# Two transposing transfers of a graph kernel, each made in two halves, with a product that waits for each half

## The chip, the cores and the metric

The kernel runs on one core of a Trainium2 chip. The metric is the device time of one execution in microseconds; the median of three executions of the kernel before is 1985.3 us (1983.23 to 1985.93). The engines are TensorE (matrix products), VectorE (DVE), ScalarE (ACT), GpSimd (POOL) and SyncE (SP). In this kernel SP issues every transfer.

## What is computed

128 independent graphs of 128 nodes with 512 features, in two layers, each a residual around a pre-normalised layer:

```python
# layer 0
h = max(layernorm(x), 0)
x = x + L0(h)          # D^-1/2 (A + I) D^-1/2 (h @ W + b)
# layer 1
h = max(layernorm(x), 0)
x = x + L1(h)
# L1: two hypergraph convolutions with a layer norm between them
h = relu(Dn * H (Be * H^T (h @ W1^T)) + b1)     # 512 -> 1024 features
h = layer_norm(h, gamma, beta)                  # this is hn
y = Dn * H (Be * H^T (h @ W2^T)) + b2           # 1024 -> 512 features
```

A is the adjacency matrix, H its nonzero pattern, Dn and Be the inverse degrees of nodes and of hyperedges. The step that the change touches is `h @ W2^T`: hn is 128 nodes x 1024 features, W2^T is 1024 x 512.

## The kernel before

Every float32 operand of a product is split into a float16 high part and a float16 low part, and three products stand for one: high x high, high x low, low x high. The helper `with_weights` (matmuls at L403) does this for a product with a weight matrix: three blocks, and within each one product per block of 128 features. For W2 there are eight such feature blocks, so 24 products of 128x128 by 128x512 that accumulate in the bank `ps_u`.

A product needs its left operand with features on the partitions, while hn is made with nodes on the partitions. So hn's two parts are transposed by transfers from SBUF to SBUF:

- ACT makes `hn_hi` (L675, `do_hn_hi`), DVE makes `hn_lo` (L984, `do_hn_lo`), each 128x1024 in one buffer. Both wait until the previous graph's transfer has read the buffer.
- SP issues one transposing transfer for each (L294, helper `transposed`, called by `do_trh` and `do_trl`) into `hnT_hi` and `hnT_lo`, which have a slot for even and one for odd graphs. Each slot has its semaphore, raised by 16 when the transfer has landed.
- TensorE's `do_U` waits for the high transfer ahead of its first product, and inside `with_weights`, by the argument `low`, for the low transfer ahead of the third block of eight.
- ACT and DVE evacuate `ps_u` into `uh` (L681) and `ul` (L998), and `do_Y2` (L445 to L447) multiplies by the graph's propagation matrix.

Layer 0 has the same form with half the width: `h0T_hi` and `h0T_lo` are transposed 128x512 transfers, made by the same helper, and `do_Y0` multiplies them by W.

The graphs are a software pipeline. In a steady step k TensorE works on T1 of graph k-1, Y0 of graph k, Y2 of graph k-3, two small products, Y1a, Z0 and Y1b, and last on U of graph k-2. The step function of each engine writes its order out by hand; the loop `steady` is unrolled and covers graphs 6 to 121. The opening and the end have orders of their own, also written by hand. SP's order in a steady step is: high transfer of h0 (k+1), high and low transfer of hn (k-2), low transfer of h0, store of the output (L321), load of x (L275), load of adj (L271). Each engine takes its instructions strictly in this order, and waits are on semaphores. In the opening SP's order around graph 1 is `do_tr0l(4); do_trl(1); do_trh(1); do_ldX(7); do_ldA(8); do_st(0); do_tr0h(5)`: there the low transfer of hn goes first.

Of the kernel before, what the change touches and what calls it, by code (L numbers as in the profile page):

```python
# [5 lines left out]
def bass_adjacency_prenorm_two_layer_gnn_kernel(  # L6
# [28 lines left out]
    DH = W1T.shape[1]  # L35
    CH = 512
# [23 lines left out]
    with ctx:  # L60
        def sb(name, shape, dt=F32):
            return ctx.enter_context(nc.sbuf_tensor(name, shape, dt))

        def sem(name):
            return ctx.enter_context(nc.semaphore(name))
# [31 lines left out]
        q = sb("q", [128, 2])  # L97
# [28 lines left out]
        hn_hi, hn_lo = sb("hn_hi", [128, DH], F16), sb("hn_lo", [128, DH], F16)  # L126
        hnT_hi, hnT_lo = sb("hnT_hi", [128, 2 * DH], F16), sb("hnT_lo", [128, 2 * DH], F16)
# [39 lines left out]
        s_wh = [sem(f"W{n}_hi_blocks") for n in range(3)]  # L167
        s_wl = [sem(f"W{n}_lo_blocks") for n in range(3)]
# [1 line left out]

        s_x = [sem(f"x_loaded_{m}") for m in range(4)]
        s_adj = [sem(f"adj_loaded_{m}") for m in range(4)]
        s_trh = [sem(f"hn_hi_transposed_{m}") for m in (0, 1)]
        s_trl = [sem(f"hn_lo_transposed_{m}") for m in (0, 1)]
        s_st = [sem("out_stored_0"), sem("out_stored_1")]

        s_at, s_ahat, s_ht = sem("adjT_in_psum"), sem("ahatT_ready"), sem("HT_and_count_ready")
# [28 lines left out]
        s_u, s_uh, s_ul = sem("u_in_psum"), sem("u_hi_ready"), sem("u_lo_ready")  # L206
# [6 lines left out]
        def at_step(i, k, want):  # L213
            return isinstance(i, int) and k == want
# [3 lines left out]
        def wait(eng, s, i, g):  # L218

            if not isinstance(i, int) or g >= 0:  # L220
                eng.wait_ge(s, upto(i, g))

        def settled(eng):

            eng.wait_ge(s_const, 1)
# [6 lines left out]
        def upto(i, g):  # L232

            return i + (g + 1) if isinstance(i, int) else count[g + 1]
# [15 lines left out]
        def wait_transposed(eng, pair, i, g):  # L250

            if not isinstance(i, int) or g >= 0:
                eng.wait_ge(pair[g % 2], i * 8 + 16 * (g // 2 + 1))
# [9 lines left out]
        def _(sp):  # L263
# [26 lines left out]
            def transposed(dst, g, src, loaded):  # L290

                width = src.shape[1]
                slot = dst[:, g % 2 * width:(g % 2 + 1) * width].rearrange("p (c r) -> p c r", r=128)
                sp.dma_start_transpose(slot, src[:, :]).then_inc(loaded[g % 2], 16)  # L294

            def do_trh(g, i=0):
                settled(sp)
                sp.wait_ge(s_hnh, upto(i, g))
                wait(sp, s_u, i, g - 2)
                transposed(hnT_hi, g, hn_hi, s_trh)  # L300

            def do_trl(g, i=0):
                settled(sp)
                sp.wait_ge(s_hnl, upto(i, g))
                wait(sp, s_u, i, g - 2)
                transposed(hnT_lo, g, hn_lo, s_trl)

            def do_ldA(g, i=0):
                wait(sp, s_at, i, g - 4)
# [26 lines left out]
            def step(i, k):  # L336
                do_tr0h(k + 1, i)
                do_trh(k - 2, i)
                do_trl(k - 2, i)
                do_tr0l(k + 1, i)  # L340
                do_st(k - 4, i)
                do_ldX(k + 4, i)
                do_ldA(k + 4, i)
# [22 lines left out]
            load_row(b1_all, b1, s_rows)  # L366
            do_tr0h(1); do_tr0l(1); do_ldA(4); do_ldX(4); do_tr0h(2); do_tr0l(2); do_ldX(5); do_ldA(5)
            do_trh(0); do_trl(0); do_ldX(6); do_tr0h(3); do_tr0l(3); do_ldA(6); do_tr0h(4); do_ldA(7)
            do_tr0l(4); do_trl(1); do_trh(1); do_ldX(7); do_ldA(8); do_st(0); do_tr0h(5); do_tr0l(5)
            do_trh(2); do_trl(2); do_ldX(8); do_trh(3); do_ldX(9); do_ldA(9); do_trl(3); do_tr0h(6); do_st(1)  # L370
            do_tr0l(6)
# [13 lines left out]
        def _(pe):  # L385
# [6 lines left out]
                    mm = pe.matmul(ps[:, f], lhs_lo[:, f], rhs_hi, start=False, stop=True)  # L392
                return mm

            def with_weights(ps, t_hi, t_lo, w_hi_, w_lo_, blocks, cols, first=None, low=None):

                for n, (t, w) in enumerate(((t_hi, w_hi_), (t_hi, w_lo_), (t_lo, w_hi_))):
                    if low is not None and n == 2:
                        wait_transposed(pe, *low)
                    for j in range(blocks):  # L400
                        if first is not None and n < 2:
                            pe.wait_ge(first[n], j + 1)
                        mm = pe.matmul(ps, t[:, j * 128:(j + 1) * 128], w[:, j, cols],  # L403
                                       start=(n == 0 and j == 0), stop=(n == 2 and j == blocks - 1))
                return mm
# [43 lines left out]
            def do_Y1a(g, i=0):  # L449
                pe.wait_ge(s_t1h, upto(i, g))  # L450
                pe.wait_ge(s_t1l, upto(i, g))
                pe.wait_ge(s_t1h, upto(i, g))
                pe.wait_ge(s_t1l, upto(i, g))
                with_weights(Y1[0][:, :], t1h, t1l, w1h, w1l, KI, slice(0, CH),
                             first=(s_wh[1], s_wl[1]) if at_step(i, g, 0) else None).then_inc(s_y1[0], 1)

            def do_Y1b(g, i=0):
                pe.wait_ge(s_t1h, upto(i, g))
                pe.wait_ge(s_t1l, upto(i, g))
                wait(pe, s_z[1], i, g - 1)  # L460
                with_weights(Y1[1][:, :], t1h, t1l, w1h, w1l, KI, slice(CH, 2 * CH),
                             first=(s_wh[1], s_wl[1]) if at_step(i, g, 0) else None).then_inc(s_y1[1], 1)
# [27 lines left out]

            def do_U(g, i=0):
                cols = slice(g % 2 * DH, (g % 2 + 1) * DH)
                wait_transposed(pe, s_trh, i, g)
                wait(pe, s_uh, i, g - 1)
                wait(pe, s_ul, i, g - 1)
                if at_step(i, g, 0):
                    pe.wait_ge(s_wsum[2], 1)
                with_weights(ps_u[:, :], hnT_hi[:, cols], hnT_lo[:, cols], w2h, w2l, KH, slice(0, DIN),
                             first=(s_wh[2], s_wl[2]) if at_step(i, g, 0) else None, low=(s_trl, i, g)).then_inc(s_u, 1)

            def do_Y2(g, i=0):
                r = g % 4
# [22 lines left out]
            def step(i, k):  # L525
                do_T1(k - 1, i)
                do_Y0(k, i)
                do_Y2(k - 3, i)
                do_AT(k + 2, i)
                do_P(k, i)  # L530
                do_Y1a(k - 1, i)
                do_Z0(k, i)
                do_Y1b(k - 1, i)
                do_U(k - 2, i)
# [18 lines left out]
            beta_row(range(6, 8)).then_inc(s_vps, 1)  # L553
            do_Y1a(0); do_Y1b(0); do_Y0(2); do_AT(4); do_P(2); do_T1(1); do_Z0(2); do_Y1a(1); do_Y1b(1)
            do_U(0); do_T1(2); do_Y0(3); do_Y1b(2); do_Y2(0); do_AT(5); do_Z0(3); do_P(3); do_Y1a(2); do_Y0(4)
            do_U(1); do_T1(3); do_AT(6); do_P(4); do_Z0(4); do_Y2(1); do_Y1b(3); do_Y1a(3); do_Y0(5); do_U(2)
            do_T1(4); do_P(5); do_Z0(5); do_AT(7); do_Y2(2); do_Y1b(4); do_Y1a(4); do_U(3)
            steady(pe, ENG.PE, step)
# [13 lines left out]
        def _(act):  # L572
# [95 lines left out]
            def do_hn_hi(g, i=0):  # L668
                m = g % 2
                act.wait_ge(s_ln2, upto(i, g))  # L670
                act.wait_ge(s_h[0], upto(i, g))
                act.wait_ge(s_h[1], upto(i, g))
                wait(act, s_hnl, i, g - 1)
                wait_transposed(act, s_trh, i, g - 1)
                act.activation(hn_hi[:, :], h[:, :], ACT.Identity, bias=nm2[:, m:m + 1], scale=sc2[:, m:m + 1])\  # L675
                   .then_inc(s_hnh, 1)

# [10 lines left out]
            def step(i, k):  # L688
                do_ha(k - 1, i)
                do_hb(k - 1, i)  # L690
                do_xh(k, i)
                do_xh_hi(k, i)
                do_h0_hi(k + 2, i)
                do_uh(k - 2, i)
                do_t1h(k, i)
                do_hn_hi(k - 1, i)
                do_h0(k + 2, i)
                do_rsum(k + 4, i)
                do_yh(k + 1, i)
                do_A_hi(k + 2, i)  # L700
                do_vq(k - 1, i)
                do_P_hi(k + 1, i)
# [50 lines left out]
        def _(dve):  # L753
# [226 lines left out]
            def do_hn_lo(g, i=0):  # L980
                dve.wait_ge(s_hn, upto(i, g))
                dve.wait_ge(s_hnh, upto(i, g))
                wait_transposed(dve, s_trl, i, g - 1)
                dve.tensor_tensor(hn_lo[:, :], hn[:, :], hn_hi[:, :], ALU.subtract).then_inc(s_hnl, 1)  # L984

            def do_out(g, i=0):
# [32 lines left out]
            def step(i, k):  # L1019
                do_yv(k, i)  # L1020
                do_hn_lo(k - 2, i)
                do_yl(k, i)
                do_h0_lo(k + 1, i)
# [347 lines left out]
```

## Time and profile before

| what | value |
|---|---|
| median of three executions | 1985.3 us (1983.23 to 1985.93) |
| the profiled execution, its own time | 1986.17 us |
| its span, first to last instruction | 1984.4 us |
| TensorE busy | 1961.7 us, 99% |
| DVE busy | 1727.7 us, 87% |
| POOL busy | 1249.4 us, 63% |
| ACT busy | 1083.7 us, 55% |
| W2's products (three groups of 1024) | 243.2 + 242.3 + 241.9 us |
| transposing issues of hn | 128 high, 128 low, 3.1 and 3.3 us to landing |
| mean granted TensorE clock | 0.998 |

The chain of work that ended last lies on TensorE for 98% of the span. A product of 128x128 by 128x512 is shown as 379 ns long, but products overlap: in an unbroken stream the next one starts 0.216 us after the last. So starts, not durations, are to be compared. "To landing" is counted from the start of the issue on SP to the moment at which the transfer's semaphore is complete.

### The profile page before, as it was taken

The numbers are of one execution on the slowest core, as the hardware profiler recorded it, in microseconds if no ns is written. First come the engines' busy times: TensorE is split into PE (matmuls) and PEld (weight loads), VectorE is DVE, ScalarE is ACT, GpSimd is POOL, SyncE is SP. The second block draws the span as 40 slices with busy tenths as digits, with TensorE's granted clock in tenths as the row PEclk, the third lists the DMA queues.
The fourth block names the chain that finished last, engine by engine and source line by source line (L and its number), as shares of the span: only waits on it lengthen the run. The fifth ranks groups of instructions, "written<-read, shape, count | busy, mean of one in ns | idle before, by whom it ended". The sixth has DMA issues, their size and how long they took to land.

```text
span 1984.4 us, 41182 instructions
## 1 busy us (share of the span) xinstructions
PE 1961.7 (99%) x10438; PEld 953.7 (48%) x10438; DVE 1727.7 (87%) x4516; ACT 1083.7 (55%) x2083; POOL 1249.4 (63%) x1934
## 2 busy tenths in 40 slices
PE   7999999999999999999999999999999999999998
PEld 3444444444444444444444444444444444444443
DVE  7988888888888888888888988889888898888985
ACT  6655555555555555555555555555555555555543
POOL 4566666666666666666666666666666666666563
PEclk9999999999999999999999999999999999999999
DMA  6344445444544444444444444444444444544432
GB/s 183 79 95 96 87 90 99 91 88 96 98 87 90 98 91 87 94 101 87 89 93 96 88 90 102 88 88 95 98 87 90 99 91 87 93 101 87 85 82 67
DMA packets 468152, 185.17 MB, mean 93 GB/s; under 512 B 416336, under 2 KB 432720, under 8 KB 467920
## 3 DMA queue, kind: packets, MB, share of 16 engines
q1 hardware_dynamic: 467920, 182.55, 44.9%
q8 instruction: 88, 1.44, 0.3%
q14 instruction: 144, 1.18, 0.2%
HBM read 48.24 MB, written 33.55 MB: 41 GB/s over the span
## 4 chain that ended last, share of the span: by engine, by line
PE 98%; DMA 1%; issue 0%; DVE 0%; ACT 0%; SPq 0%; POOL 0%; DVEq 0%; ACTq 0%; POOLq 0%
PE ps_u L403 34%; PE ps_c L403 33%; PE ps_e L403 16%; PE ps_c L390 1%; PE ps_c L392 1%; PE ps_c L391 1%; PE ps_e L445 1%; PE ps_y L445 1%; PE ps_e L446 1%; PE ps_e L447 1%; PE ps_y L447 1%; PE ps_y L446 1%; PE ps_a L480 1%; PE ps_p L488 0%; PE ps_p L489 0%
## 5 line engine op out<-in xcount | busy, mean ns | idle before, releaser
L599 ACT ACTIVATE h<-z 128x512 f32<-128x512 f32 x256 | 160.8, 629 | 540.2 <-DVE z L792 540.2
L1188 POOL TENSOR_TENSOR rd<-u,neg_half 128x2 f32<-128x2 f32 x128 | 180.9, 1413 | 248.9 <-DVE y L1009 224.5
L403 PE MATMUL ps_c<-w1h,t1h 128*128 128x512 f16 x1024 | 263.7, 380 | 0.9 <-DVE t1l L953 0.9
L403 PE MATMUL ps_c<-w1l,t1h 128*128 128x512 f16 x1024 | 262.9, 379 | 0.0
L403 PE MATMUL ps_c<-w1h,t1l 128*128 128x512 f16 x1024 | 262.8, 379 | 0.0
L403 PE MATMUL ps_u<-w2h,hnT_hi 128*128 128x512 f16 x1024 | 243.2, 380 | 0.0
L403 PE MATMUL ps_u<-w2l,hnT_hi 128*128 128x512 f16 x1024 | 242.3, 379 | 0.0
L403 PE MATMUL ps_u<-w2h,hnT_lo 128*128 128x512 f16 x1024 | 241.9, 379 | 0.0
L1234 POOL TENSOR_TENSOR scr<-x1b,xh 128x512 f32<-128x512 f32 x128 | 229.2, 1791 | 0.3
L1169 POOL TENSOR_TENSOR base<-scr,vq 128x512 f32<-128x512 f32 x128 | 223.4, 1745 | 7.9 <-ACT vq L593 4.4
L792 DVE SCALAR_TENSOR_TENSOR z<-ps_c,dn,b_all 128x512 f32<-128x512 f32 x256 | 191.0, 746 | 29.4 <-PE ps_c L403 29.2
L1009 DVE SCALAR_TENSOR_TENSOR y<-b_sc,rd,ps_e 128x512 f32<-128x512 f32 x128 | 95.6, 747 | 136.2 <-PE ps_e L403 136.1
L1208 POOL TENSOR_TENSOR u<-st,eps_t 128x1 f32<-128x1 f32 x128 | 25.6, 200 | 266.5 <-DVE st L895 266.4
L681 ACT ACTIVATE uh<-ps_u 128x512 f16<-128x512 f32 x128 | 76.4, 597 | 214.1 <-PE ps_u L403 213.9
L1228 POOL TENSOR_TENSOR x1b<-x,b_all 128x512 f32<-128x512 f32 x128 | 165.0, 1289 | 2.7 <-DVE x L884 2.5
L797 DVE BATCH_NORM_STATS2 raw<-h 128x6 f32<-128x512 f32 x256 | 161.4, 670 | 2.3 <-ACT h L599 2.2
L675 ACT ACTIVATE hn_hi<-h,nm,sc 128x1024 f16<-128x1024 f32 x128 | 157.7, 1232 | 4.1 <-POOL nm L1283 4.0
L403 PEld LDWEIGHTS ps_u<-w2l,hnT_hi 128*128 128x128 f16 x1024 | 100.3, 98 | 121.5 <-issue 1.1
L403 PEld LDWEIGHTS ps_u<-w2h,hnT_hi 128*128 128x128 f16 x1024 | 100.3, 98 | 121.5 <-issue 1.1
L403 PEld LDWEIGHTS ps_c<-w1l,t1h 128*128 128x128 f16 x1024 | 100.3, 98 | 121.2 <-issue 0.8
L403 PEld LDWEIGHTS ps_c<-w1h,t1l 128*128 128x128 f16 x1024 | 100.2, 98 | 120.8
L403 PEld LDWEIGHTS ps_u<-w2h,hnT_lo 128*128 128x128 f16 x1024 | 100.2, 98 | 120.9
(124 smaller groups left out, 4431.5 us busy)
## 6 DMA issues: line engine op xcount, KB each, us to landing
x_t<-in_x_dram SPq DMA_DIRECT2D x128, 256.0 KB, 2.9
out_dram<-out_t SPq DMA_DIRECT2D x128, 256.0 KB, 2.3
adj_t<-in_adj_dram SPq DMA_DIRECT2D x128, 64.0 KB, 2.6
raw_w<-in_W1T_dram SPq DMA_DIRECT2D x4, 512.0 KB, 8.4
h0T_hi<-h_hi SPq DMA_TRANSPOSE x128, 2.4
h0T_lo<-h_lo SPq DMA_TRANSPOSE x128, 2.5
raw_w<-in_W2T_dram SPq DMA_DIRECT2D x8, 256.0 KB, 4.9
hnT_hi<-hn_hi SPq DMA_TRANSPOSE x128, 3.1
```

The source lines that it names most:

```text
L403: mm = pe.matmul(ps, t[:, j * 128:(j + 1) * 128], w[:, j, cols], start=(n == 0 and j == 0), stop=(n == 2 and j == blocks - 1))
L445: pe.matmul(ps, lhs_hi, rhs_hi, start=True, stop=False)
L599: act.activation(h[:, cols], z[:, cols], ACT.Relu).then_inc(s_h[n], 1)
L675: act.activation(hn_hi[:, :], h[:, :], ACT.Identity, bias=nm2[:, m:m + 1], scale=sc2[:, m:m + 1])\
L681: act.activation(uh[:, :], ps_u[:, :], ACT.Copy, scale=U_EVAC).then_inc(s_uh, 1)
L792: dve.scalar_tensor_tensor(out=z[:, cols], in0=Y1[n][:, :], scalar=dn1[:, m:m + 1], in1=b1_all[:, cols], op0=ALU.mult, op1=ALU.add).then_i ...
L797: dve.bn_stats(raw2[:, n, :], h[:, n * CH:(n + 1) * CH]).then_inc(s_rw2[n], 1)
L1009: dve.scalar_tensor_tensor(out=y[:, :], in0=b_sc[:, :], scalar=rd0[:, m, 1:2], in1=Y0[:, :], op0=ALU.mult, op1=ALU.add).then_inc(s_y, 1)
L1169: pool.tensor_tensor(base2[:, m, :], scr2[:, m, :], vq[:, :], ALU.add).then_inc(s_base2, 1)
L1188: pool.tensor_tensor(rd0[:, m, :], u0[:, m, :], neg_half[:, :], ALU.pow).then_inc(s_pp0, 1)
L1228: pool.tensor_tensor(x1b[:, :], x1[:, g % 2, :], b2_all[:, :], ALU.add).then_inc(s_x1b, 1)
L1234: pool.tensor_tensor(scr2[:, g % 2, :], x1b[:, :], xh[:, :], ALU.add).then_inc(s_scr2, 1)
```

## The change

Each of hn's two transposing transfers becomes two, of four feature blocks each (128x512), issued one right after the other. Each half has its own pair of semaphores. TensorE waits for the first high half ahead of product 0 of its first block, for the second high half ahead of product 4 of that block, and for the two low halves ahead of products 0 and 4 of the third block. ACT and DVE wait for both halves of the previous graph before they overwrite `hn_hi` and `hn_lo`. h0's transfers are as before.

```diff
-        s_trh = [sem(f"hn_hi_transposed_{m}") for m in (0, 1)]
-        s_trl = [sem(f"hn_lo_transposed_{m}") for m in (0, 1)]
+        s_trh = [[sem(f"hn_hi_half{q}_transposed_{m}") for m in (0, 1)] for q in (0, 1)]
+        s_trl = [[sem(f"hn_lo_half{q}_transposed_{m}") for m in (0, 1)] for q in (0, 1)]
...
+            def transposed_halves(dst, g, src, pair):
+
+                for q in (0, 1):
+                    at = g % 2 * DH + q * CH
+                    sp.dma_start_transpose(dst[:, at:at + CH].rearrange("p (c r) -> p c r", c=CH // 128),
+                                           src[:, q * CH:(q + 1) * CH]).then_inc(pair[q][g % 2], 16)
+
             def do_trh(g, i=0):
                 settled(sp)
                 sp.wait_ge(s_hnh, upto(i, g))
                 wait(sp, s_u, i, g - 2)
-                transposed(hnT_hi, g, hn_hi, s_trh)
+                transposed_halves(hnT_hi, g, hn_hi, s_trh)
...
-                transposed(hnT_lo, g, hn_lo, s_trl)
+                transposed_halves(hnT_lo, g, hn_lo, s_trl)
...
                     for j in range(blocks):
+                        if halves is not None and n == 0 and j == blocks // 2:
+                            wait_transposed(pe, halves[0][1], *halves[2:])
+                        if halves is not None and n == 2 and j % (blocks // 2) == 0:
+                            wait_transposed(pe, halves[1][2 * j // blocks], *halves[2:])
...
             def do_U(g, i=0):
                 cols = slice(g % 2 * DH, (g % 2 + 1) * DH)
-                wait_transposed(pe, s_trh, i, g)
+                wait_transposed(pe, s_trh[0], i, g)
...
-                             first=(s_wh[2], s_wl[2]) if at_step(i, g, 0) else None, low=(s_trl, i, g)).then_inc(s_u, 1)
+                             first=(s_wh[2], s_wl[2]) if at_step(i, g, 0) else None, halves=(s_trh, s_trl, i, g)).then_inc(s_u, 1)
...
                 wait(act, s_hnl, i, g - 1)
-                wait_transposed(act, s_trh, i, g - 1)
+                wait_transposed(act, s_trh[0], i, g - 1)
+                wait_transposed(act, s_trh[1], i, g - 1)
...
-                wait_transposed(dve, s_trl, i, g - 1)
+                wait_transposed(dve, s_trl[0], i, g - 1)
+                wait_transposed(dve, s_trl[1], i, g - 1)
```

## Rows read from the trace of the kernel before

**Rows 1.** The page, part 1: busy us (share of the span) and instructions.

```profile
PE 1961.7 (99%) x10438; PEld 953.7 (48%) x10438; DVE 1727.7 (87%) x4516; ACT 1083.7 (55%) x2083; POOL 1249.4 (63%) x1934
```

**Rows 2.** Windows: from:to, length, busy us (instructions) of each engine, PEclk, DMA, GB/s.

```profile
60.00:105.00 45.00, 45.00 (x242) 21.52 (x240) 41.57 (x111) 24.95 (x48) 24.90 (x42) 1.00 0.42 84
...
112.00:1955.00 1843.00, 1842.95 (x9855) 897.67 (x9854) 1620.12 (x4236) 1008.41 (x1939) 1180.62 (x1818) 1.00 0.45 92
1955.00:1985.00 30.00, 21.64 (x99) 9.08 (x97) 12.76 (x19) 7.35 (x10) 8.96 (x15) 0.90 0.28 70
```

**Rows 3.** Timeline of TensorE, W2's products of a steady step: start, us, instruction.

```profile
1012.33 1.89 PE L403 MATMUL ps_u<-w2h,hnT_hi 128*128 128x512 f16 x8
...
1015.79 1.89 PE L403 MATMUL ps_u<-w2h,hnT_lo 128*128 128x512 f16 x8
1017.51 0.22 PE L390 MATMUL ps_c<-P_hi,xh_hi 128*128 128x128 f16 x1
```

**Rows 4.** Timeline of the SP queue, the issues of the same step.

```profile
1005.04 1.23 SPq L294 DMA_TRANSPOSE hnT_hi<-hn_hi  x1
1007.78 1.23 SPq L294 DMA_TRANSPOSE hnT_lo<-hn_lo  x1
1009.12 1.22 SPq L294 DMA_TRANSPOSE h0T_lo<-h_lo  x1
...
1011.53 0.39 SPq L271 DMA_DIRECT2D adj_t<-in_adj_dram  x1
1016.09 1.20 SPq L294 DMA_TRANSPOSE h0T_hi<-h_hi  x1
```

**Rows 5.** DMA issues, us to landing: medians of all, then the one issued at 72.16.

```profile
h0T_hi<-h_hi SPq DMA_TRANSPOSE x128, 2.4
hnT_hi<-hn_hi SPq DMA_TRANSPOSE x128, 3.1
...
hnT_hi<-hn_hi SPq DMA_TRANSPOSE x1, 3.1
```

**Rows 6.** Timeline of the SP queue around graph 1.

```profile
70.84 1.23 SPq L294 DMA_TRANSPOSE hnT_lo<-hn_lo  x1
72.16 1.29 SPq L294 DMA_TRANSPOSE hnT_hi<-hn_hi  x1
73.56 0.52 SPq L275 DMA_DIRECT2D x_t<-in_x_dram  x1
...
74.59 0.43 SPq L321 DMA_DIRECT2D out_dram<-out_t  x1
78.07 1.20 SPq L294 DMA_TRANSPOSE h0T_hi<-h_hi  x1
```

**Rows 7.** Timelines of weight loads and products, W2's first block of graph 1.

```profile
75.64 1.61 PEld L403 LDWEIGHTS ps_u<-w2h,hnT_hi 128*128 128x128 f16 x8
...
75.85 1.89 PE L403 MATMUL ps_u<-w2h,hnT_hi 128*128 128x512 f16 x8
```

**Rows 8.** Timelines of the last two graphs: SP issue, products, a weight load.

```profile
1959.17 1.24 SPq L294 DMA_TRANSPOSE hnT_hi<-hn_hi  x1
...
1962.95 1.89 PE L403 MATMUL ps_u<-w2h,hnT_hi 128*128 128x512 f16 x8
...
1971.78 0.58 PEld L403 LDWEIGHTS ps_u<-w2h,hnT_hi 128*128 128x128 f16 x4 [0.38 <-DMA hnT_hi<-hn_hi]
```

**Rows 9.** Timeline of TensorE after an idle time; 11 products start from 50.73 on.

```profile
50.73 0.58 PE L445 MATMUL ps_e<-yh,A_hi 128*128 128x512 f16 x1 [1.20 <-DVE yl L1016]
...
54.67 1.03 PE L403 MATMUL ps_c<-w1h,t1l 128*128 128x512 f16 x4
```

**Rows 10.** Windows: PEclk in the stretch after that idle time.

```profile
52.00:54.00 2.00, 2.00 (x6) 0.69 (x5) 1.97 (x3) 2.00 (x4) 2.00 (x2) 0.51 0.71 135
```

**Rows 11.** Timeline of TensorE, two neighbouring starts in step 3.

```profile
83.08 0.38 PE L447 MATMUL ps_y<-uh,P_lo 128*128 128x512 f16 x1
83.32 1.02 PE L403 MATMUL ps_c<-w1h,t1h 128*128 128x512 f16 x4
```

More of the change, by code:

```diff
@@ L393, in aggregate, with with_weights @@
                 return mm
-            def with_weights(ps, t_hi, t_lo, w_hi_, w_lo_, blocks, cols, first=None, low=None):
+            def with_weights(ps, t_hi, t_lo, w_hi_, w_lo_, blocks, cols, first=None, low=None, halves=None):
                 for n, (t, w) in enumerate(((t_hi, w_hi_), (t_hi, w_lo_), (t_lo, w_hi_))):
```

## The prediction, made before the result was known

> **What bounds the kernel now.** I read the share of each engine first: TensorE is busy 1961.7 of 1984.4 us [rows 1]. Then I cut the span into stages to see where the missing 22.7 us lie [rows 2]. The reader is to see that none fall between 60 and 105, 0.05 between 112 and 1955, and at most 8.4 after 1955 (30.00 less 21.64, a window that reaches a little past the end); what is left, some 15, lies before 60 us but for a trifle between 105 and 112. The granted clock is 1.00 from 60 to 1955, the 2.4 GHz level. So from 60 us on the kernel is one unbroken stream of products, and any time by which that stream stops is added to the end; any other engine's time is free until it stops that stream.
>
> The third view is the timeline of a steady step on TensorE and on the SP queue [rows 3, 4]. The three blocks of W2's products start at 1012.33 (the first) and 1015.79 (the third), and the next work at 1017.51: 3.46 us for two blocks and 1.72 for one, 0.216 for each of the 24 products. A wait for the low transfer stands already ahead of the third block, and it leaves no trace in these starts. The transfers were issued at 1005.04 and 1007.78. With 3.1 us to landing [rows 5] they are there at 1008.1 and 1010.9, 4.2 and 4.9 us before those two starts. A split transfer cannot start TensorE earlier here, since TensorE is never waiting for it.
>
> **The change part by part.** (a) *Two more issues per step on SP.* One issue of hn's full width lasts 1.23 us, one of h0's half the width lasts 1.20 [rows 4, 6]. The width does not set this price, so a half costs what a whole costs. Two transposing issues stand 1.34 us apart start to start (1007.78 to 1009.12) [rows 4]. The change adds 2 x 1.34 = 2.68 us of SP work per step. Steady step: the high halves go out at 1005.04 and 1006.38, the second ending at 1007.61, just before the 1007.78 at which the low part is ready, so this 1.34 falls into a wait that was there. The low halves go out at 1007.78 and 1009.12; all behind them (h0's low transfer, the store, the x and adj loads) moves back by 1.34. The last, the adj load at 1011.53, ends near 1013.3 instead of 1011.9, and the next issue is due at 1016.09 [rows 4]: 2.8 us of air. Without that air the stream would begin to slip by what is over. h0's low transfer would land at 1013.0 and is used in the step after 1017.51. Cost: 0.
>
> (b) *When the halves land.* The nearest row is h0's transposing transfer, the same 128x512 shape: 2.4 us; the other end is the whole one's 3.1 [rows 5]. I take 2.5, by the row of the same shape. Steady step: the second high half lands at 1006.38 + 2.5 = 1008.9, the second low one at 1011.6; they are wanted 0.86 us (four products) after 1012.33 and after 1015.79, that is at 1013.2 and 1016.7. Hidden, even at 3.1. Cost: 0.
>
> (c) *The waits.* TensorE passes four waits per graph instead of two, DVE and ACT one more each before they overwrite hn's two halves of the split. For a wait already satisfied the two ends are 0 (no gap at 1015.79 [rows 3]) and 0.02 us, the gap ahead of a product at 83.32, where the stream would have gone on at 83.30 [rows 11]. I take 0, because the row at 0 is this very kind of wait at this very place. Behind a TensorE wait the whole stream queues; behind the ACT and DVE waits stands work with no claim on the end, and the transfers they ask for landed most of a step before.
>
> (d) *The one place where the order is tight.* In the opening, graph 1's transfers go out low first, then high: 70.84 and 72.16 [rows 6]. The high one lands at 72.16 + 3.1 = 75.26; its first weight load is at 75.64 and its first product at 75.85 [rows 7]. The spare time is 0.38 us. Now three issues stand ahead of the last high half instead of one. The high halves go out at 70.84 + 2 x 1.34 = 73.52 and at 74.86. The first lands at 76.02 and product 0 starts at 76.05 (0.03 between load and product is my estimate; a starved load has no lead over its product), against 75.85: 0.20 late. Product 4 was due at 75.85 + 4 x 0.216 = 76.71; the second half lands at 77.36 and it starts at 77.39: 0.68 late in all, the first delay included. Bounds: spacing 1.25 and landing 2.4 give 70.84 + 3.75 + 2.4 + 0.03 = 77.02, 0.31 late; spacing 1.37 and landing 3.1 give 78.08, 1.37 late. (1.25 and 1.37 are estimates, 0.09 below and 0.03 above the measured 1.34.) I take 0.68. From here to 1955 TensorE has no slack to win this back, so it goes to the end. The issues behind (x, adj, a store) begin near 76.2 instead of 73.56 and took 1.5 us before (73.56 to 75.02), so they finish near 77.7, against 78.07 for the next transposing one [rows 6]. Cost: 0.
>
> The Trainium skill speaks against this change in "DMA: Bandwidth & Descriptors", section "Rules for kernel authors": small transfers are to be coalesced into one large one. Its section "Anatomy of one DMA" gives a fixed part of about 2.0 us and bytes/436e3 on top (fitted on the other issuing path). If that fixed part were paid one transfer after another, the estimate for the second high half would be 76.02 + 2.3 = 78.3 and the delay 1.6 us. The trace is against the serial reading: the transfer issued at 72.16, 1.32 after another of its size, lands in its 3.1 us, the median of all 128 [rows 5, 6]; it did not wait for the one ahead.
>
> (e) *The other tight places.* Near the end graph 126's high transfer goes out at 1959.17 and its products start at 1962.95: the second half lands at 1960.51 + 2.5 = 1963.0, wanted for product 4 at 1963.8. Hidden. Graph 127's weight load at 1971.78 had waited 0.38 us for the transfer [rows 8], but a load runs 0.21 ahead of its product when nothing holds it (75.64 and 75.85 [rows 7]), so the products gain at most 0.38 - 0.21 = 0.17 from a first half that lands 0.6 earlier, at 1971.2; I take 0.1. The second half, issued 1.34 later, lands at 1972.5, and product 4 is due at 1971.7 + 0.86 = 1972.6 at the earliest, later if the clock is low there (0.90 in the mean after 1955 [rows 2]). Cost: 0, up to 0.6 with the landing of 3.1.
>
> **Sum.** +0.68 (d) - 0.1 (e) = +0.6. The profiled execution took 1986.17 us (span 1984.4 and 1.8 around it): 1986.8. The median of the runs is 0.87 lower, so 1985.3 + 0.6 = **1985.9 us**.
>
> **Rivals.** *A, the clock falls at graph 1.* For: after 1.20 us of idleness at 50.73 the next 11 products took until 54.67, 3.94 us against 11 x 0.216 = 2.38, and between 52 and 54 the granted clock was 0.51, the 1.2 GHz level [rows 9, 10]. Price 1.56, in all +2.2: 1987.5. Against: here there are two gaps of about 0.2 and 0.5 us after 15 us without one.
>
> *B, nothing stands still at graph 1.* The last half must land by 76.71, so three spacings may take 76.71 - 2.53 - 70.84 = 3.34, 1.11 each instead of 1.34: a half would have to issue in about 1.0 us. Only the gain of 0.1 is left: 1985.2. Against it stands the 1.20 of h0's issues [rows 6].
>
> *C, slower: the new waits in mid-stream.* Place: the fourth product of W2's first and third block, on TensorE's queue. Price by the gap of 0.02 us [rows 11]: 2 new places x 128 graphs x 0.02 = 5.1, with the 0.6 above 1991.0. It decides from 0.013 us a wait (3.4 / 256). Against: the zero at 1015.79.
>
> *D, faster: the products start earlier.* It needs a TensorE that waits for hn's transfers. That is so once, for at most 0.17 us of products [rows 8]; and the 8.4 us after 1955 [rows 2] are the most that anything there could give. To gain 4 us nothing in the profile offers a place; should later issues happen to thin out DMA traffic, up to 5 us: 1980.5.
>
> **How the numbers follow.** Forecast (a stall of 0.3 to 1.4 us at graph 1) 0.70; A 0.09; B 0.12; C 0.06; D 0.03. The measurement tells about 0.2%, 4 us, from no change. Forecast, A and B all lie within it: same 0.90 (their 0.91, less a little for scatter), slower 0.07, faster 0.03. The range: the runs before scatter from 1983.23 to 1985.93. With B and the forecast's low end it starts at 1983.3; with A, the upper bound 1.4 and scatter it ends at 1988.8; C and D stay out.
>
> **What the profile after would show.** Four issues of hn per graph at about 1.2 us, hn's landings near 2.5; TensorE's idle list with two entries at graph 1 for the high transfer, together 0.3 to 1.4 us, and no other new one; W2's blocks in the steady step still 1.73 apart; SP's last issue of a step about 1.3 later. I am wrong if a half issues in 1.0 us or less, if W2's blocks stretch beyond 1.73, if the stretch 112 to 1955 no longer is full for TensorE, or if the clock drops between 76 and 80 us.

## The result, and the profile after

The changed kernel takes 1988.91 us (median of 20 executions, 1987.04 to 1990.51), the kernel before 1985.49 (20 executions, 1983.09 to 1986.61). The ratio is 1.0019, 95% interval 1.0013 to 1.0025: 3.4 us slower by the medians, 2.6 to 5.0 us by the interval. The forecast was 1985.9 with a range of 1983.3 to 1988.8; the direction was right (slower), the size was not: +3.4 us where +0.6 was forecast, and 0.1 us above the range.

The page of the changed kernel, part 1, its windows (columns as in rows 2), and its transposing issues of hn with us to landing:

```profile
PE 1961.3 (99%) x10438; PEld 953.4 (48%) x10438; DVE 1731.7 (87%) x4516; ACT 1083.5 (55%) x2083; POOL 1249.3 (63%) x1934
```

```profile
60.00:105.00 45.00, 43.69 (x232) 20.47 (x231) 40.59 (x105) 23.97 (x47) 24.95 (x41) 1.00 0.37 82
105.00:112.00 7.00, 6.81 (x34) 2.96 (x32) 6.01 (x18) 3.54 (x6) 5.03 (x9) 1.00 0.69 98
112.00:1955.00 1843.00, 1842.02 (x9858) 897.76 (x9858) 1621.30 (x4237) 1008.38 (x1939) 1182.69 (x1823) 1.00 0.43 92
```

```profile
hnT_hi<-hn_hi SPq DMA_TRANSPOSE x256, 2.5
hnT_lo<-hn_lo SPq DMA_TRANSPOSE x256, 2.5
```

TensorE's busy time is the same as in [rows 1] to 0.4 us. What is new is idle time: 1.31 us between 60 and 105, where [rows 2] had none, and 0.98 between 112 and 1955, where they had 0.05.

The loop is not where it lies. W2's blocks of a steady step:

```profile
1014.93 1.89 PE L414 MATMUL ps_u<-w2h,hnT_hi 128*128 128x512 f16 x8
1016.66 1.89 PE L414 MATMUL ps_u<-w2l,hnT_hi 128*128 128x512 f16 x8
1018.38 1.89 PE L414 MATMUL ps_u<-w2h,hnT_lo 128*128 128x512 f16 x8
```

They are 1.73 and 1.72 us apart, as in [rows 3], with four real waits instead of two. The first idle place is graph 1. The SP queue, the weight loads and the products there, to be set beside [rows 6, 7]:

```profile
71.47 2.50 SPq L300 DMA_TRANSPOSE hnT_lo<-hn_lo  x2
74.10 2.50 SPq L300 DMA_TRANSPOSE hnT_hi<-hn_hi  x2
76.71 0.51 SPq L275 DMA_DIRECT2D x_t<-in_x_dram  x1
...
78.65 1.23 SPq L294 DMA_TRANSPOSE h0T_hi<-h_hi  x1
```

```profile
76.62 0.55 PEld L414 LDWEIGHTS ps_u<-w2h,hnT_hi 128*128 128x128 f16 x4 [0.46 <-DMA hnT_hi<-hn_hi]
77.86 0.55 PEld L414 LDWEIGHTS ps_u<-w2h,hnT_hi 128*128 128x128 f16 x4 [0.70 <-DMA hnT_hi<-hn_hi]
```

```profile
76.62 1.04 PE L414 MATMUL ps_u<-w2h,hnT_hi 128*128 128x512 f16 x4
77.87 1.04 PE L414 MATMUL ps_u<-w2h,hnT_hi 128*128 128x512 f16 x4 [0.21 <-DMA hnT_hi<-hn_hi]
```

Both halves are waited for. Product 4 starts 1.25 us after product 0 instead of 0.86. The bracket shows only 0.21 of it: a product's shown 0.38 us overlaps the next by 0.16, so a start-to-start gap is larger than the idle time printed.

The second place was in no step of the prediction. SP, DVE and TensorE of the changed kernel around T1 of graph 3:

```profile
87.06 2.52 SPq L300 DMA_TRANSPOSE hnT_hi<-hn_hi  x2
89.69 2.52 SPq L300 DMA_TRANSPOSE hnT_lo<-hn_lo  x2
92.32 0.52 SPq L275 DMA_DIRECT2D x_t<-in_x_dram  x1
```

```profile
95.15 0.69 DVE L868 BATCH_NORM_STATS2 raw<-x_t 128x6 f32<-128x512 f32 x1 [1.38 <-DMA x_t<-in_x_dram]
...
97.82 0.68 DVE L912 SCALAR_TENSOR_TENSOR xh_lo<-xh,xh_hi 128x512 f16<-128x512 f32 x1
```

```profile
98.61 0.22 PE L397 MATMUL ps_c<-P_hi,xh_hi 128*128 128x128 f16 x1 [1.01 <-issue]
```

and the same load of x (graph 8) and the same DVE instruction before:

```profile
88.64 0.52 SPq L275 DMA_DIRECT2D x_t<-in_x_dram  x1
```

```profile
91.86 0.69 DVE L856 BATCH_NORM_STATS2 raw<-x_t 128x6 f32<-128x512 f32 x1
```

Before, the load lands at 88.64 + 2.9 = 91.5, 0.3 us before DVE takes it up: no wait. After, it is issued 3.68 us later (2.5 for the two more issues in front of it, 1.16 that the queue was late already at h0's low transfer, 85.77 against 84.61), DVE stands for 1.38 us with xh_lo queued behind, and T1 needs xh_lo. The trace names "issue" as the cause at T1; the cause is found one engine further, in DVE's own waits; the runs below test it.

The third place is near the end, at Y0 of graph 124:

```profile
1887.30 2.50 SPq L300 DMA_TRANSPOSE hnT_hi<-hn_hi  x2
1889.91 2.73 SPq L300 DMA_TRANSPOSE hnT_lo<-hn_lo  x2
1892.76 1.19 SPq L294 DMA_TRANSPOSE h0T_lo<-h_lo  x1
```

```profile
1889.57 0.38 PE L456 MATMUL ps_e<-yh,A_hi 128*128 128x512 f16 x1 [0.42 <-DVE yl L1029]
...
1895.24 1.04 PE L414 MATMUL ps_e<-w0h,h0T_lo 128*128 128x512 f16 x4 [0.55 <-DMA h0T_lo<-h_lo]
```

h0's low transfer waits behind four halves of hn and lands at 1895.2 for products that were due at 1894.5.

**The account.** "Lateness" below is the start of a product less the start of the same product in the kernel before, less that difference at 63.4 us. In the changed kernel it is 0.53 us at 81 us, 1.70 at 96, 1.96 at 109, then constant to 0.1 us through the 1770 us of the loop, and 3.06 from 1898 to the last wait of TensorE at 1971. In the two profiled executions two more differences cancel part of it: 0.64 us at 63 us, and the last graph's W2 products, which ran at the lower clock in the kernel before and at the upper one after:

```profile
1972.00:1974.00 2.00, 2.00 (x7) 0.75 (x6) 0.68 (x1) 0.00 (x0) 0.00 (x0) 0.56 0.76 251
```

```profile
1975.00:1977.00 2.00, 2.00 (x11) 0.93 (x10) 0.75 (x1) 0.00 (x0) 0.67 (x2) 1.00 0.50 99
```

(before, then after, graph 127's first block in both). Both kernels stand idle 2.14 us just ahead of it, so this is no work of the change; that is why the spans differ by 2.0 us only.

### The profile page after: what moved, and what is told of

It reads as the page before. It is cut to its first block and busy times, and to the rows that moved or that the text cites. A ratio compares the mean times of both kernels' runs of the same rounds, so it can differ in the third digit from the quotient of the medians.

```text
span 1986.4 us, 41693 instructions
## 1 busy us (share of the span) xinstructions
PE 1961.3 (99%) x10438; PEld 953.4 (48%) x10438; DVE 1731.7 (87%) x4516; ACT 1083.5 (55%) x2083; POOL 1249.3 (63%) x1934
## 3 DMA queue, kind: packets, MB, share of 16 engines
q14 instruction: 148, 1.21, 0.2%
```

## The experiments

The theory (S) was that the loss comes from SP's queue outside the loop, in the three places above; the rival (L) was a cost in every graph of the loop. Time ratios are to the kernel before, timed beside each run, with 95% intervals; lateness is defined above.

| kernel | ratio | late at 81 | at 96 | at 109 | at 1898 |
|---|---|---|---|---|---|
| changed, result | 1.0019 (1.0013 to 1.0025) | 0.53 | 1.70 | 1.96 | 3.06 |
| changed again | 1.0018 (1.0009 to 1.0027) | 0.53 | 1.71 | 1.96 | 3.03 |
| halves in the loop only | 1.0007 (0.9998 to 1.0015) | 0.00 | 0.00 | -0.01 | 0.26 |
| halves outside the loop only | 1.0016 (1.0007 to 1.0025) | 0.53 | 1.76 | 2.01 | 3.36 |
| SP's order mended | 0.9999 (0.9990 to 1.0008) | 0.00 | 0.00 | 0.00 | 0.36 |
| graph 1's high part first | 1.0014 (1.0004 to 1.0023) | -0.01 | 1.30 | 1.57 | 2.64 |
| x load of graph 8 first | 1.0009 (1.0000 to 1.0018) | 0.53 | 0.53 | 0.54 | 2.55 |
| order near the end | 1.0009 (1.0000 to 1.0018) | 0.53 | 1.93 | 2.19 | 2.56 |
| more waits only | 1.0003 (0.9994 to 1.0011) | -0.01 | -0.01 | 0.00 | 0.01 |

**The changed kernel again** (no edit).

> The changed kernel once more, unaltered, for a second trace. Theory S (SP's queue order outside the loop): the changed kernel stops TensorE in three hand-written places and nowhere in the loop: at graph 1's W2 products for hn's high halves (0.53 us more than before), ahead of T1 of graph 3 (1.01 us), because the load of x for graph 8 stands behind three more issues and DVE waits for it, and near the end at h0's low transfer of graph 124 (0.55 us). These places must return in this trace with the same sizes to 0.1 us. Rival L (a cost per graph in the loop): W2's blocks are farther apart than 1.73 us or the loop's steps longer than 15.13 us. Rival O (chance in the opening): the 0.5 us by which the profiled changed kernel is late already at 48.7 us, before any transfer of hn, comes and goes between traces. Expected time: ratio to the kernel before 1.0013 to 1.0025.

The three places return with the same sizes to 0.03 us of lateness. What changes is the opening (it is 0.75 us earlier at 63 us than in the first trace of the changed kernel) and the end (the granted clock is 0.61 and 0.53 in graph 127's first block). Across the nine traces of the table and that of the kernel before, the start at 63 us varies by 2.0 us, with no order by what was changed: rival O holds.

**Halves in the loop only, and outside it only.** One predicate decides which graphs are halved; the waits follow it.

```diff
+        def halved(g):
+            return LOOP_FROM - 2 <= g < LOOP_TO - 2        # the complement: not ...
...
-                transposed_halves(hnT_hi, g, hn_hi, s_trh)
+                if halved(g):
+                    transposed_halves(hnT_hi, g, hn_hi, s_trh)
+                else:
+                    transposed(hnT_hi, g, hn_hi, s_trh[0])
```

> Halves for graphs 4 to 119, those whose transfers the loop issues; whole transfers for graphs 0 to 3 and 120 to 127. 116 of 128 graphs keep the change. Theory S: the three stops are gone, the time is that of the kernel before to within 0.4 us (the place at h0's low transfer near the end may stay if it comes from the loop's last steps, 0.6 us). Rival L: nearly all of the loss stays, +3 us, ratio 1.0015 or more.

> The complement: halves for graphs 0 to 3 and 120 to 127 only, 12 of 128 graphs. Theory S: nearly all of the loss stays, +2 to +3.5 us, with the same three stops in the trace. Rival L: +0.3 us (12/128 of the loss), no stop of TensorE that the kernel before hasn't.

12 graphs of 128 carry the loss: 1.0016 and 3.36 us of lateness, against 0.26 for the other 116. L is out. The 3.36 are 0.3 more than in the changed kernel: the stop near the end is 1.36 us here instead of 0.73, with graph 121's two high issues taking 3.38 us instead of 2.50, and the wait for yl in front of it is not there.

The kernel with halves in the loop alone is not quite the kernel before: its lateness rises to 1.23 us by 1955, in two steps of 0.66 and 0.30 near 1917 and 1941 us, more than the 0.4 us expected. Its interval includes both no change and 1.0015. Of the other traces only that of the quarters in the loop (below) has these steps, 0.69 and 0.30. Both kernels have split transfers in the loop and whole ones behind it. Ahead of the first step DVE, in both, stands 0.4 us instead of 0.05 before an aggregate and then takes 1.74 us instead of 0.81 for hn. The profile names no transfer there, and the cause stays open.

**SP's order mended in three places.**

```diff
-            do_tr0l(4); do_trl(1); do_trh(1); ...
+            do_tr0l(4); do_trh(1); do_trl(1); ...
-            do_trh(2); do_trl(2); do_ldX(8); ...
+            do_ldX(8); do_trh(2); do_trl(2); ...
-            ... do_trh(NG - 7); do_trl(NG - 7); do_tr0l(NG - 4); do_st(NG - 9)
-            do_ldX(NG - 1); do_ldA(NG - 1); ...
+            ... do_trh(NG - 7); do_tr0l(NG - 4); do_ldX(NG - 1); do_trl(NG - 7); do_st(NG - 9)
+            do_ldA(NG - 1); ...
```

> All halves as in the changed kernel, but SP's order outside the loop mended in three places: graph 1's high transfer ahead of its low one, the load of x for graph 8 ahead of graph 2's transfers, and near the end h0's low transfer of graph 124 and the load of x for graph 127 ahead of graph 121's low transfer. Theory S: the stops of 0.53, 1.01 and 0.55 us go, so 2.1 us are won against the changed kernel, and the time is within 1 us of the kernel before. Rival L: the time stays at +3 us and more.

All 128 graphs are halved and the loss is gone: 0.9999, lateness 0.36. What is left is TensorE's 0.4 us wait for yl ahead of graph 123's Z0. It is 0.27 to 0.38 us late there in every kernel whose loop is halved and 0 where it isn't, so it belongs to the loop's halves. It enters on DVE, 5 us earlier: DVE stands 0.55 us instead of 0.20 ahead of an aggregate (L985; L973 before) in all of them but the kernel with halves in the loop only, where it stands 0.41 instead of 0.06 one instruction later. DVE's waits for hn's halves stand elsewhere, ahead of hn_lo, and the profile names no transfer here; why DVE stands longer was not found.

**Each of the three alone.**

> The changed kernel with one edit: graph 1's high transfer ahead of its low one on SP. Theory S: TensorE's stop at graph 1's W2 products (0.14 and 0.39 us) goes, the others stay: 0.5 us less of lateness against the kernel before between 63 and 105 us. If step (d) of the prediction were the whole loss, the time would be back at the kernel before; by theory S 2.5 us of the loss stay.

> The changed kernel with one edit: the load of x for graph 8 ahead of graph 2's transfers on SP. Theory S: DVE's wait of 1.38 us for this load goes, and with it TensorE's stop ahead of T1 of graph 3 (1.17 us of lateness) and the 0.26 us that follow until 109 us: 1.4 us less than the changed kernel. The stop at graph 1 stays at 0.53. Rival: the stop ahead of T1 has another cause (a store of instructions, DVE's added wait) and stays.

> The changed kernel with the edit near the end alone: h0's low transfer of graph 124 and the load of x for graph 127 ahead of graph 121's low transfer. Theory S: the stop of 0.55 us (0.73 of lateness) at Y0 of graph 124 goes, the opening stays as in the changed kernel. The wait of 0.4 us for yl ahead of it stays, as in the kernel with all three edits.

Each edit removes its own stop and leaves the others. With graph 1's stop gone (-0.01 at 81 us) 2.64 of 3.06 us stay: the step that the prediction had taken for the whole is a sixth of the loss. The next stop is 0.14 us larger than in the changed kernel. The five traces in which the load of x stays behind have it at 1.17, 1.18, 1.24, 1.31 and 1.40 us, in step with the load's own time to landing, 2.81, 2.81, 2.87, 2.95 and 3.04 us; so this is the load's scatter and nothing that the edit did. With the x load first, the load goes out at 85.55 and DVE takes it without a wait:

```profile
85.55 0.52 SPq L275 DMA_DIRECT2D x_t<-in_x_dram  x1
```

```profile
92.18 0.68 DVE L868 BATCH_NORM_STATS2 raw<-x_t 128x6 f32<-128x512 f32 x1
```

Lateness stays at 0.53 to 0.54 through 109 us: this load was 1.43 us of the loss. A rival cause is at hand: DVE's hn_lo of graph 2, which stands ahead of DVE's use of x, takes 2.28 us instead of 1.22 in the changed kernel. The traces rule it out: with the x load first it takes 2.29 and T1 does not stop, with graph 1's high part first it takes 1.22 and T1 stops all the same. Near the end the stop at h0's low transfer is 1.48 us in this trace, not 0.55, because one of graph 121's issues there took 2.2 us instead of 1.2; so this kernel's total misses the expected gain by 0.9. With the end's order alone that stop is gone and the lateness stays at 2.56. (This edit also moves the x load of graph 127 forward; it is the trace that puts the stop down to h0's low transfer.) The times of 10 executions do not tell these three kernels from the changed one, since their intervals overlap its own; only the traces do.

**The waits by themselves.**

```diff
                     for j in range(blocks):
+                        if hi is not None and n == 0 and j == blocks // 2:
+                            wait_transposed(pe, *hi)
+                        if hi is not None and n == 2 and j == blocks // 2:
+                            wait_transposed(pe, *low)
```

> The kernel before with whole transfers; TensorE waits four times per graph instead of two, twice for the same landed transfer, at the places where the changed kernel waits for the second halves. Measures the new waits by themselves. Theory S: 0 (1.73 us between W2's blocks, time within 0.3 us of the kernel before). Rival C of the prediction: 0.02 us a wait, +5.1 us.

Nothing: 0.01 us of lateness over the whole execution. This kernel has only one instruction more than the kernel before (41183 to 41182), so a second wait for an event already waited for may have left no instruction behind. The changed kernel's own W2 blocks, with waits for events of their own and still 1.73 us apart, are the better evidence against rival C.

**Quarters in the loop**, to see where SP's air ends. Each half is issued as two quarters that raise one semaphore; graphs outside the loop are whole.

```diff
-                for q in (0, 1):
-                    at = g % 2 * DH + q * CH
-                    sp.dma_start_transpose(dst[:, at:at + CH].rearrange("p (c r) -> p c r", c=CH // 128),
-                                           src[:, q * CH:(q + 1) * CH]).then_inc(pair[q][g % 2], 16)
+                for q in range(4):
+                    at = g % 2 * DH + q * 256
+                    sp.dma_start_transpose(dst[:, at:at + 256].rearrange("p (c r) -> p c r", c=2),
+                                           src[:, q * 256:(q + 1) * 256]).then_inc(pair[q // 2][g % 2], 16)
```

> The loop's graphs (4 to 119) in quarters: eight issues of hn per graph instead of two, still two waits for each part on TensorE (the quarters of a half raise one semaphore). The others whole. Theory S: an issue costs 1.2 to 1.3 us whatever its width, so from the first high issue to the landing of the last low one it is 7 x 1.31 + 2.3 = 11.5 us, and TensorE gives 11.4 to 11.6: the loop is at its limit. Either still no loss in the loop, or a stop of 0.1 to 0.3 us in each of its 116 graphs at the low transfer, +12 to +35 us. Rival (an issue's price goes with its width, 0.6 us for a quarter): no stop and no loss.

The median is 2187.08 us, ratio 1.1013 (1.0997 to 1.1028): 202 us slower, where 0 to 35 was expected. The price of an issue was right; the place was wrong again. SP, DVE and TensorE in one step:

```profile
1008.95 5.04 SPq L313 DMA_TRANSPOSE hnT_hi<-hn_hi  x4
1014.13 5.03 SPq L313 DMA_TRANSPOSE hnT_lo<-hn_lo  x4
1019.27 1.80 SPq L307 DMA_TRANSPOSE h0T_lo<-h_lo  x1
1021.12 0.58 SPq L347 DMA_DIRECT2D out_dram<-out_t  x1
1021.80 0.36 SPq L288 DMA_DIRECT2D x_t<-in_x_dram  x1
```

```profile
1009.08 0.69 DVE L887 BATCH_NORM_STATS2 raw<-x_t 128x6 f32<-128x512 f32 x1 [3.83 <-DMA x_t<-in_x_dram]
```

```profile
1011.71 0.38 PE L475 MATMUL ps_y<-uh,P_hi 128*128 128x512 f16 x1 [2.00 <-issue]
```

```profile
DVE raw L887 <- DMA x_t<-in_x_dram: 317.7, 108, 6.2
...
PE ps_y L475 <- issue: 118.5, 87, 3.3
```

The last two rows are waits of the whole execution: us in total, times, the longest. Not the low transfer (6.2 us of TensorE's idle time) but the x load at the tail of SP's step holds DVE back, 108 times, and ul, queued behind it on DVE, holds TensorE's Y2. Against the kernel before TensorE is idle 126 us more and busy 68 us more; the mean granted clock is 0.987 instead of 0.998. SP is not simply full: it still stands 229 us waiting for ACT's hn_hi (368 before), and the x load comes behind that wait in its order. All this is read from the waits; no kernel with quarters and the x load moved forward was run. So the loop seems to have the same weak place as the opening. Its margin in one step of the two kernels follows from one row each of DVE, the first before, the second after:

```profile
1016.39 0.69 DVE L856 BATCH_NORM_STATS2 raw<-x_t 128x6 f32<-128x512 f32 x1
```

```profile
1018.98 0.68 DVE L868 BATCH_NORM_STATS2 raw<-x_t 128x6 f32<-128x512 f32 x1
```

Before, the load issued at 1011.07 lands at 1013.8, 2.6 us early. After, it is issued at 1015.49 and lands at 1018.1, 0.9 us early. Over the loop's steps the margin is 2.4 us at the median and 0.8 at the least before, and 0.8 at the median after. In four steps after, DVE does wait for this load, 0.9 us in all and at most 0.3, and TensorE still does not stop. So the halves ate two thirds of the margin, and they cost nothing in the loop by a small one only.

**Halves where TensorE waits for them.** Only graph 127 is halved, and at the end DVE makes graph 126's ul before graph 127's hn_lo.

```diff
-            ... do_hn(NG - 1); do_hn_lo(NG - 1)
-            do_out(NG - 3); do_ul(NG - 2); do_out(NG - 2); ...
+            ... do_hn(NG - 1); do_out(NG - 3)
+            do_ul(NG - 2); do_hn_lo(NG - 1); do_out(NG - 2); ...
```

> Halves where TensorE does wait for hn, the last graph, and whole transfers for the other 127. One edit beside it on DVE at the very end: the order output of graph 125, low part of uh's split of graph 126, hn_lo of graph 127, instead of hn_lo first. In the kernel before TensorE stands 2.14 us for that split (ul) and then finds graph 127's high transfer just landing at 1971.8. Theory S: Y2 of graph 126 starts 0.7 us earlier, graph 127's first high half lands 0.7 us earlier, so its W2 products start at about 1971.0: 0.7 us faster than the kernel before, up to 2.4 us if the shorter idle time keeps the granted clock at its upper level there (in the profiled kernel before it was 0.56 to 0.59 from 1972 to 1976, price 1.7 us). Rival: no gain, because graph 127's low halves, issued after hn_lo 1.8 us later, come too late for the third block.

> The same edit on DVE alone, all transfers whole. Theory S: Y2 of graph 126 starts 0.7 us earlier, but W2's products of graph 127 still wait for the whole high transfer at 1971.8: no gain to the kernel before but through the clock, and the difference to the kernel with graph 127 halved is what the half is worth, 0.7 us.

> The kernel with only the last graph halved and DVE's order at the end changed, once more, to narrow its interval. Theory S: 0.7 us from the earlier start of graph 127's W2 products and up to 1.7 us from the granted clock, in all 1 to 2 us under the kernel before. Rival: the 1.3 us by which its median was lower the first time was scatter.

Ratios 0.9995 (0.9986 to 1.0004) and 0.9998 (0.9989 to 1.0007) with the half, 0.9999 (0.9990 to 1.0008) without it: no gain that these runs can tell, where 0.7 to 2.4 us were expected of the half; the two medians are 1.3 and 0.3 us below the kernel before. The traces show what the half does. Graph 126's Y2 and graph 127's W2 products with the half, then with whole transfers:

```profile
1968.96 0.38 PE L470 MATMUL ps_y<-uh,P_hi 128*128 128x512 f16 x1 [1.52 <-DVE ul L1025]
...
1969.61 2.18 PE L428 MATMUL ps_u<-w2h,hnT_hi 128*128 128x512 f16 x8
...
1974.57 1.04 PE L428 MATMUL ps_u<-w2h,hnT_lo 128*128 128x512 f16 x4 [0.19 <-DMA hnT_lo<-hn_lo]
```

```profile
1969.86 0.38 PE L445 MATMUL ps_y<-uh,P_hi 128*128 128x512 f16 x1 [1.52 <-DVE ul L998]
...
1971.03 1.90 PE L403 MATMUL ps_u<-w2h,hnT_hi 128*128 128x512 f16 x8 [0.36 <-DMA hnT_hi<-hn_hi]
```

TensorE waits 1.52 us for ul instead of 2.14, and the W2 products follow Y2's start by 0.65 us with the half and by 1.17 without: 0.5 us for the half, once in 1985. The rival's late low half takes part of it back: by the last products 0.24 us are left between the two traces.

## Why the prediction was wrong

- **What bounds the kernel**: right. TensorE's stream without gaps, every stop carried to the end; 1.96 us of lateness at 109 us arrives at 1886 us undiminished.
- **(a), the price of an issue**: right at the median. Two halves take 2.50 us and stand 1.31 to 1.32 apart on average, against 1.34 assumed; SP's last issue of a step is 1.3 us later, as forecast. Not forecast were the long ones: 22 of the 512 halves and 33 of h0's 128 low transfers behind them last over 1.5 us, up to 2.4, against 4 of 256 and none before.
- **(a), "Cost: 0" for all that stands behind the added issues**: here is the failure. The test was when SP's next issue is due, not when the engine that uses each delayed transfer needs it, and it was made in the steady step and, at the end of (d), behind graph 1. There it held: h0's next transfer goes out at 78.65, which is 78.0 less the 0.64 us of the opening, against 78.07. It was never made at graphs 2 and 121. At graph 2 the x load had 0.3 us of margin to DVE's use and was pushed by 2.5: 1.43 us. Near the end h0's low transfer had 1.5 us of margin and was pushed by 2.2, past its use: 0.73 us. 0.37 more come with the loop's halves, from a cause that stays open. Together 2.5 of the 3.06 us. In the loop "Cost: 0" held, but the spare time was the 2.4 us to DVE's use of x, not the 2.8 to SP's next issue.
- **(b), landings**: right. 2.5 us at the median, for 256 high and 256 low halves.
- **(c), waits at no cost**: right for TensorE, by the blocks of 1.73 us. That DVE's work has no claim on the end was wrong at graph 2, where xh_lo and with it TensorE's T1 stood behind DVE's wait for x.
- **(d), the stop at graph 1**: right in place and kind. 0.68 was forecast, within 0.31 to 1.37; it is 0.53 in all five traces with this order.
- **(e), the tight places near the end**: graph 126 hidden, as forecast. The gain of 0.1 at graph 127 cannot be read apart from the clock.
- **Sum**: +0.6 forecast, +3.06 by lateness, +3.4 by the medians. The mis-sized term is the 0 of (a): 2.2 us by the two stops that the edits remove, 2.5 with the 0.37 of open cause. The remaining 0.4 between lateness and medians is within what the opening and the clock at the end do from one execution to the next.
- **Rivals**: A, B, C and D are all out. The granted clock is 1.00 from 60 to 105 us through both stops. The chance of 0.9 for no change that can be told went by a bound of 0.2%: the measured 0.19% lies just inside it, but its interval leaves out no change.
- **Signs of being wrong**: one came true, the stretch from 112 to 1955 is no longer full for TensorE. Its 0.98 us lie at 1889 and 1895, behind the loop, and no part in it. The list of TensorE's idle times also has new entries beside graph 1's.

The Trainium skill's rule to coalesce small transfers ("DMA: Bandwidth & Descriptors", "Rules for kernel authors") pointed the right way, although a half is 128 KB here and the rule speaks of mostly overhead under 64 KB. A fixed part of a transfer's time, as the Trainium skill's "Anatomy of one DMA" gives it for the other issuing path, may well be in these landings too (2.4 us for 128x256, 2.5 for 128x512, 3.1 for 128x1024), but halves issued 1.24 us apart land 2.5 us after their issues each, so it is not paid one after another. What the kernel paid for was the 1.2 us of SP's time per issue, and it was paid by what stood behind in the queue.

## What to carry to other kernels

When a queue gets more issues, list every transfer behind them on that queue, in every stretch that has an order of its own, and take each one's margin to its consumer, not to the queue's next issue. A transposing transfer had its price on the issuing queue by the piece and not by its width (1.2 us at 256, 512 and 1024 columns), so cutting one in two can only pay where the consumer does wait for it. A stop that the profile puts down to "issue" is followed up in the waits of the engine whose result is missing.

## What the runs showed that I had not expected

- Cutting further has a cliff: two issues more per graph cost the loop nothing, six more cost 10%. The margin of the x load is 2.4 us at the median before and 0.8 with the halves.
- At the median the issue of a quarter (128x256) lasts 1.24 us, of a half 1.21 (high) and 1.25 (low), of a whole 1.23.
- After TensorE's 2.14 us of idleness at the end the granted clock is at its upper level through graph 127's three blocks in three traces (the changed kernel's first, SP's order mended, quarters) and falls to 0.50 within them in the eight others, the changed kernel's second among them. After 1.52 us, in the three traces with DVE's order at the end changed, it was 1.00.
